# Self-attention values on 32x32 diagonal tiles with a row-sum column, in a one-layer perceiver kernel

## What is computed

```python
def _L0_attn_ref(x, ...):              # B = 128, L = 32, D = 256, H = 16 heads, HD = 16
    q = rms_norm(x, qn_scale) @ q_w.T + q_b
    k = rms_norm(x, kn_scale) @ k_w.T + k_b
    v = x @ v_w.T + v_b
    ...                                 # split in heads, rotary on q and k
    scores = jnp.einsum('bhqd,bhkd->bhqk', q, k) * scale
    weights = jax.nn.sigmoid(scores)
    weights = weights / (jnp.sum(weights, axis=-1, keepdims=True) + EPS_RENORM)
    attn = jnp.einsum('bhqk,bhkd->bhqd', weights, v)
    attn = attn.transpose(0, 2, 1, 3).reshape(B, L, D)
    return attn @ o_w.T + o_b
```

## Time and profile before

| | before |
|---|---|
| median of 3 runs | 1345.84 us (1345.80 to 1345.89) |
| the profiled execution | 1344.86 us |
| its span in the trace | 1343.0 us |
| one body in the steady part | 36.73 us |
| busy in the span: PE, DVE, ACT, POOL | 86%, 70%, 65%, 42% |

### The profile page before, as it was taken

One profiled execution on the slowest core, in us unless ns is written; L12 is line 12 of the kernel. 1 busy time (PEld: TensorE's weight loads), 2 busy tenths in 40 slices (PEclk: granted clock), 3 DMA queues, 4 the chain that ended last, 5 costly groups with the idle time before them and its releaser, 6 DMA issues.

```text
span 1343.0 us, 37302 instructions
## 1 busy us (share of the span) xinstructions
PE 1157.5 (86%) x14033; PEld 936.5 (70%) x14033; DVE 945.0 (70%) x2523; ACT 872.4 (65%) x2443; POOL 569.7 (42%) x1045
## 2 busy tenths in 40 slices
PE   6898889888888898889888888988898888864797
PEld 5676777767767777777767767767777677742697
DVE  3667777777777777777777777877777777763121
ACT  3676767777777667767777777667677777632131
POOL 1244454455444444444454444444444554431121
PEclk9899999999999999999999999999999999975899
DMA  6414211111211111111111111111111111000474
GB/s 148 126 47 144 84 57 43 51 54 51 52 40 45 49 52 47 50 47 39 46 48 50 49 30 50 49 49 46 50 40 39 48 48 45 14 9 13 115 225 153
DMA packets 71904, 81.93 MB, mean 61 GB/s; under 512 B 16987, under 2 KB 50732, under 8 KB 71728
## 3 DMA queue, kind: packets, MB, share of 16 engines
q1 hardware_dynamic: 65280, 75.19, 19.3%
q0 software_dynamic: 3200, 3.71, 0.8%
q10 hardware_dynamic: 3248, 0.66, 0.2%
HBM read 64.79 MB, written 16.56 MB: 61 GB/s over the span
## 4 chain that ended last, share of the span: by engine, by line
DVE 33%; PE 31%; ACT 20%; issue 9%; POOL 6%; SPq 0%; DVEq 0%; DMA 0%; ACTq 0%; POOLq 0%
ACT prob L739 8%; ACT wbd L799 4%; PE score L444 4%; PE vps L411 4%; PE kps L401 4%; DVE prob L974 4%; ACT qz L728 3%; DVE nmx L963 3%; PE shared L477 3%; PE shared L532 3%; PE shared L523 3%; PE score L670 3%; PE score L684 3%; DVE pr L1116 3%; POOL ctx_p L1273 2%
## 5 line engine op out<-in xcount | busy, mean ns | idle before, releaser
L739 ACT ACTIVATE prob<-score,nmx 128x257 f32<-128x257 f32 x512 | 236.2, 476 | 175.8 <-DVE nmx L963 175.0
L401 PE MATMUL kps<-ctx_p,wk_p 128*128 128x256 f32 x1536 | 213.6, 289 | 0.2 <-POOL ctx_p L1273 0.2
L411 PE MATMUL vps<-wv_p,ctx_p 128*128 128x256 f32 x1536 | 212.7, 288 | 0.0
L1273 POOL TENSOR_TENSOR ctx_p<-ctxT,ctx_p 128x512 fp32r<-128x512 f32 x128 | 152.1, 1188 | 119.8 <-ACT ctx_p L755 119.8
L411 PEld LDWEIGHTS vps<-wv_p,ctx_p 128*128 128x128 f32 x1536 | 192.6, 192 | 12.4 <-issue 12.4
L401 PEld LDWEIGHTS kps<-ctx_p,wk_p 128*128 128x128 f32 x1536 | 195.4, 192 | 5.4 <-issue 2.3
L963 DVE TENSOR_REDUCE nmx<-score 128x2 f32<-128x514 f32 x256 | 163.1, 679 | 15.7 <-PE score L428 15.7
L1291 POOL TENSOR_TENSOR plast<-const,prob 128x128 f32<-128x128 f32 x128 | 64.1, 501 | 257.7 <-DVE prob L974 257.7
L974 DVE TENSOR_SCALAR prob<-prob,rsum 128x257 f32<-128x257 f32 x512 | 158.3, 352 | 9.0
L444 PE MATMUL score<-const,prob 128*128 128x128 f32 x1024 | 145.7, 280 | 7.5 <-DVE prob L974 3.5
L444 PEld LDWEIGHTS score<-const,prob 128*128 128x128 f32 x1024 | 114.1, 142 | 44.4 <-DVE prob L974 28.6
(11 more groups left out here) (163 smaller groups left out, 2188.4 us busy)
## 6 DMA issues: line engine op xcount, KB each, us to landing
ctxT<-in_ctxT SPq DMA_DIRECT2D x128, 257.0 KB, 3.0
w<-in_w SPq DMA_DIRECT2D x16, 1024.0 KB, 9.7
xq<-in_x SPq DMA_DIRECT2D x32, 128.0 KB, 3.3
xr<-in_x SPq DMA_DIRECT2D x32, 128.0 KB, 2.5
qbd<-qkT SPq DMA_DIRECT2D x256, 16.0 KB, 1.8
out<-row SPq DMA_DIRECT2D x32, 128.0 KB, 1.9
slots<-row SPq DMA_DIRECT2D x10, 257.0 KB, 5.6
x_a<-slots SPq DMA_DIRECT2D x8, 129.0 KB, 2.1
```

Of the source, the lines that this page charges most:

```text
L401: last = mm(kps[:, c, :], wk_p[:, x, n, c * P:(c + 1) * P], ctx_p[:, g, y, n, :], start=(n, x) == (0, LO), stop=(n, y) == (C - 1, LO))
L411: last = mm(vps[:, c, :], ctx_p[:, g, x, n, c * P:(c + 1) * P], wv_p[:, y, n, :], start=(n, x) == (0, LO), stop=(n, y) == (C - 1, LO))
L739: last = af(prob[:, m, :], score[:, m, 0:S], ACT.Exp, bias=nmx[:, m:m + 1], scale=1.0, accum_out=esum[:, m:m + 1])
L1273: g.tensor_tensor(ctx_p[:, g_, LO, :, :], ctxT[:, r, :, g_, 0:SM], ctx_p[:, g_, HI, :, :].bitcast(F32), ALU.subtract).then_inc(s["ctx_part ...
```

## The change

The block-diagonal matrix `wbd`, the sums by ones and the selection of even and odd heads go. `v2` becomes `v2a`: for each head 16 values and a column of ones. PE multiplies, for each head and each sequence, the 32x32 block of `th` (the weights are loaded from it as it stands) with the 32x17 block of `v2a` on the diagonal tile (rows 32j, columns 32j of the array) and gets, with tokens on partitions, the 16 values and the sum of each head in 17 columns of `shared`. DVE adds the epsilon, inverts 128x16 sums and multiplies (`att2n`). PE transposes `att2n` into `spare`, and ACT copies it to `att2`, from where the projection goes on as before.

```diff
-            def weight_sums(t):
-                pe.wait_ge(s["sig_done"], TB * (t + 1))
...
-            def weighted_values2(t):
+            def self_values(t):
+                pe.wait_ge(s["sig_flat"], t + 1)
                 pe.wait_ge(s["v2_done"], t + 1)
...
+                for h in range(H):
+                    for j in range(TB):
+                        rows = slice(32 * j, 32 * j + 32)
+                        last = mm(shared[rows, h * (HD + 1):(h + 1) * (HD + 1)], th[rows, h * L:(h + 1) * L], v2a[rows, h, :],
                                   start=True, stop=True)
                 last.then_inc(s["pv2_ps"], 1)
...
-                    (1, 2): s2 and (lambda: (turn("sm_step", 2 * (t2 + 1)), weight_sums(t2))),
-                    (1, 3): s2 and (lambda: (turn("ext2_step", 2 * (t2 + 1)), weighted_values2(t2))),
+                    (1, 2): s2 and (lambda: (turn("att2n_done", t2 + 1), self_values(t2))),
                     (2, 0): s1 and (lambda: (turn("qk_done", t1 + 1), project_qk(t1))),
+                    (2, 1): s2 and (lambda: (spare_free(xa, i, 2), transpose_rows(att2n, "att2n_done", t2, "at2_ps", spare_c))),
...
             # ScalarE
-                    if j == 2 and s2:
-                        act.wait_ge(s["o2_ps"], t2)
-                        even_heads(att2, sh_pair[:, :, 0, :], "pv2_ps", t2 + 1, "ext2_step")
-                    if j == 1 and s2:
-                        sigmoid_blocks(t2, (2,))
+                    if j == 2 and s2:
+                        act.wait_ge(s["o2_ps"], t2)
+                        copy_rows(att2[:, :, :], spare_c, "at2_ps", t2, "att2_done")
-                    if j == 0 and s2:
-                        sigmoid_blocks(t2, (0, 1))
...
             # VectorE
-            def sigmoid_block(t, j):
-            def sums2(t):
-            def extract2(t):
...
+            def inverse2(t):
+                dve.wait_ge(s["pv2_ps"], t + 1)
+                v.tensor_scalar(ssum[:, :], sh_heads[:, :, HD], 2e-8, None, ALU.add).then_inc(s["ssum_step"], 1)
+                dve.wait_ge(s["ssum_step"], 2 * t + 1)
+                v.reciprocal(rsum2[:, :], ssum[:, :]).then_inc(s["ssum_step"], 1)
+            def weigh2(t):
+                dve.wait_ge(s["ssum_step"], 2 * t + 2)
+                dve.wait_ge(s["at2_ps"], t)
+                v.tensor_tensor(att2n[:, :].rearrange("p (h d) -> p h d", d=HD), sh_heads[:, :, 0:HD],
+                                rsum2[:, :].unsqueeze(2).to_broadcast([P, H, HD]), ALU.mult).then_inc(s["att2n_done"], 1)
```

More of the change, by code:

```diff
@@ L142, in build @@
         qbd2 = sb("qbd2", [P, C, HH, P])
-        v2 = sb("v2", [P, D])
+        v2a = sb("v2a", [P, H, HD + 1])
         th, tabs, sneg = (sb(n, [P, 2 * D]) for n in ("th", "tabs", "sneg"))
-        wbd = sb("wbd", [P, H, P])
-        ssum, att2 = sb("ssum", [P, C, P]), sb("att2", [P, C, P])
+        ssum, rsum2 = sb("ssum", [P, H]), sb("rsum2", [P, H])
+        att2n, att2 = sb("att2n", [P, D]), sb("att2", [P, C, P])
         row = sb("row", [P, ROW])
@@ L188, in build @@
         counts = gather[:, 0, 0, 0:E]
-        sh_pair = shared[:, :].rearrange("p (c g n) -> p c g n", c=C, g=2)
+        sh_heads = shared[:, 0:H * (HD + 1)].rearrange("p (h d) -> p h d", d=HD + 1)
         names = """const_in wq_in wkv_in weights_in bf_consts scaled zeroed klast_done vlast_done last_ps
@@ L517, in scores2 @@
                 last.then_inc(s["s2_ps"], 1)
-            def weight_sums(t):
-                pe.wait_ge(s["sig_done"], TB * (t + 1))
-                for c in range(C):
-                    for g in range(4):
-                        last = mm(shared[32 * g:32 * g + 32, c * D:(c + 1) * D], k["ones"][:, 0:32],
-                                  wbd[:, 8 * c + 2 * g:8 * c + 2 * g + 2, :].rearrange("p h n -> p (h n)"),
-                                  start=True, stop=True)
-                last.then_inc(s["sm_ps"], 1)
-            def weighted_values2(t):
-                pe.wait_ge(s["v2_done"], t + 1)
-                for c in range(C):
-                    for g in range(4):
-                        last = mm(shared[32 * g:32 * g + 32, c * D:(c + 1) * D], v2[:, c * P + 32 * g:c * P + 32 * g + 32],
-                                  wbd[:, 8 * c + 2 * g:8 * c + 2 * g + 2, :].rearrange("p h n -> p (h n)"),
+            def self_values(t):
+                pe.wait_ge(s["sig_flat"], t + 1)
+                pe.wait_ge(s["v2_done"], t + 1)
+                if once(t):
+                    pe.wait_ge(s["zeroed"], 2)
+                for h in range(H):
+                    for j in range(TB):
+                        rows = slice(32 * j, 32 * j + 32)
+                        last = mm(shared[rows, h * (HD + 1):(h + 1) * (HD + 1)], th[rows, h * L:(h + 1) * L], v2a[rows, h, :],
                                   start=True, stop=True)
@@ L790, in sigmoid_exp @@
                 af(sneg[:, :], sneg[:, :], ACT.Exp, scale=float(-SCALE)).then_inc(s["sneg_exp"], 1)
-            def sigmoid_blocks(t, batches):
-                if once(t):
-                    act.wait_ge(s["zeroed"], 2)
-                act.wait_ge(s["sig_flat"], t + 1)
-                for j in batches:
-                    b = slice(32 * j, 32 * j + 32)
-                    af(wbd[b, :, b], th[b, :].rearrange("p (h q) -> p h q", h=H), ACT.Copy).then_inc(s["sig_done"], 1)
             def gate_exp(t):
@@ L912, in setup @@
                     v.memset(qbd2[:], 0.0).then_inc(s["zeroed"], 1)
[L913 removed]
+                    v.memset(v2a[:, :, HD:HD + 1], 1.0).then_inc(s["zeroed"], 1)
                 if j == 1:
@@ L1162, in body @@
                         norm1(t1)
-                    if j == 2 and s2:
-                        weigh2(t2)
                     if j == 2 and s1:
@@ L1179, in body @@
                         residual1(t1)
-                    if j == 1 and s2:
-                        sigmoid_block(t2, 3)
-                        sums2(t2)
                     if j == 2 and s1:
@@ L1200, in body @@
                     if j == 1 and s2:
-                        inverse2(t2, 0)
-                        extract2(t2)
-                        inverse2(t2, 1)
+                        inverse2(t2)
+                        weigh2(t2)
                     if j == 2 and s2:
```

27 lines of the change are left out of this document (5 added, 22 removed).

## The result

The changed kernel takes 1335.20 us, the median of 5 runs (1330.20 to 1336.11), beside 1345.89 us of 5 runs of the kernel before (1345.80 to 1346.71). The ratio is 0.9907, with a 95% interval of 0.9884 to 0.9930: faster by 10.7 us, where the forecast was 1300, faster by 45.6. The sign holds, and the size does not.

What follows compares the result with a forecast made beforehand. A ring of waits, with no engine full, was taken to bound the kernel; 1.36 us in each of 30 bodies (40.8) plus the drain made 45.6 us, giving 1300 us. The range of 8 in 10 was 1278 to 1338.

Steps and rivals of the forecast that it cites:

- The ring of waits: Steady body of 36.74 us: no engine fills it (PE 32.80), so what counts is which engine is late at which step.
- the walk: From the new step to L1030 in a steady body: 1.36 us earlier, carried on by an untouched 7.06 us to L483.
- Its rule: Steady body: the gain is 3.41 us less the length of the new step, 1.36 us with a step of 2.05.
- the length of the step: PE, new step to L444: 128 matmuls at 14.8 ns plus 0.15 for the change of form, 2.05 us.
- DVE's additions: DVE before L492: addition, inversion (0.25) and product, some 0.95 us with gaps, ending at 693.5 before L492 at 694.01.
- the drain: Last two bodies, clock at half: gains of 1.4 us in the body before last and 3.4 in the last.
- the start: Work up to the first step of the loop: the forecast gave it no gain, and the removed memset no price.
- a floor from start to start: New step: about 25 ns per matmul, so 3.35 us; a body gains 0.06, about 1340 us; chance 0.12.
- Serial tiles: New step: diagonal tiles go one after the other, 5.0 us; a body loses 1.6, 1402 us; chance 0.08.
- Slow issue: New step: PE's instructions come too slowly for a burst of 256, costing 0.7 us a body; 1321 us; chance 0.12.
- The short step: New step: 17 columns make it 1.36 us or less; a body gains 2.05, 1278 us; chance 0.08.
- the cap of 2.05: Gain of a body in us with a step of 1.36 or less, where ACT sets L770 at 691.54.

Runs made afterwards that it cites:

- again: The changed kernel itself, not one instruction different, run once more on another chip: 1281.8 us, ratio 0.9526.
- the memset: The changed kernel with the removed zeroing of `wbd` (128x2048) put back on DVE in the first body, its tile unused: 1287.9 us.
- split: The changed kernel with its step in two halves, heads 8 to 15 moved behind the transposes of batch 1: 1275.4 us, ratio 0.9477.
- half_heads: The changed kernel with heads 8 to 15 left out of the new step, 64 matmuls instead of 128: 1263.9 us.
- Q: A chip with long gaps: the changed kernel took 1336.2 us there, and with its step in two halves 1301.8 (single runs).
- R: A chip with long gaps: the changed kernel took 1342.2 us there, and with its step in four pieces 1291.5 (single runs).

## Why the prediction was right and wrong

**What bounds the kernel: right.** The ring of waits was read rightly, and the walk through it holds. Its rule, that a body gains 3.41 us less the length of the step, gives 0.92 for the step of 2.49 and was measured at 36.73 - 35.75 = 0.98; for the 1.70 of again it gives 1.71, measured 36.73 - 34.93 = 1.80. The exponentials start 0.79 us after DVE's first maxima do (652.01), as foreseen 0.7, and the maxima of batch 2 wait for L428 and the evacuation of q and k for L492 (again, ACT and DVE):

```profile
652.80 0.48 ACT L734 ACTIVATE prob<-score,nmx 128x257 f32<-128x257 f32 x1 [1.20 <-DVE nmx L945]
...
659.17 0.17 DVE L1039 TENSOR_SCALAR ssum<-shared 128x16 f32<-128x16 f32 x1
659.37 0.25 DVE L1041 RECIPROCAL rsum<-ssum 128x16 f32<-128x16 f32 x1
659.66 0.42 DVE L1046 TENSOR_TENSOR att2n<-shared,rsum 128x256 f32<-128x256 f32 x1
660.80 1.29 DVE L945 TENSOR_REDUCE nmx<-score 128x2 f32<-128x514 f32 x2 [0.72 <-PE score L428]
662.36 0.75 DVE L1012 SCALAR_TENSOR_TENSOR qk<-shared,rrms,r_qk 128x512 f32<-128x512 f32 x1 [0.27 <-PE shared L492]
```

**DVE's additions: right.** 0.25 us was taken for the inversion of 128x16 and is what it takes; all three end at 660.08, 0.6 before L492. The transposes and the copy of `att2n` cost nothing beside a cross-attention, as said: PE waits for them 1.0 and 1.3 us in the whole span, in the drain.

**The length of the step: the term that was mis-sized.** It was taken as 2.05 us of steady matmuls. It is 8.5 ns for each matmul, near the lower end (14.8 ns of L459, halved for fewer columns), plus gaps: 1.70 us with the short ones and 2.49 with the long ones. The forecast's own band for the step, 1.5 to 2.6, held both. With 2.49 in the rule the sum is 30 x 0.92 + 4.8 = 32.4, a time of 1313, and 13 of the 35 us of the miss are explained.

**The term that wasn't there: the granted clock.** The prediction looked at the clock only in the drain and let the steady part run at the full level because it had done so before. On the chip of the result it fell behind the new step in 22 of 29 bodies, and some 29 us went there. This is the step that failed: a term of 29 us that the sum had at nothing. With the 13 above, less 5.7 and 0.8 that the start and the drain gave beyond the forecast, it makes the 35 us. That 1335.2 lies inside the range of 1278 to 1338 is luck, since the upper end of the range stood for a floor from start to start, which the rows refute. The rows of before could have raised the question, for PE is busy for 32.80 of the 36.74 us of a body, and a stretch at half speed lengthens it. They couldn't give the answer, since the same instructions keep the full clock on three of the six chips.

**The drain and the start.** The drain was put at 4.8 us and gives 5.6. The last body gains 5.4 (from L515 to L477 14.6 us before, 9.2 after) and not 3.4, in part since the step at half clock takes 2.9 us to the transposes and not 4.1; the last body with a cross-attention, with its gaps and its stretch at 1.2 GHz, loses 1.3. The start was given nothing and gives 5.7; the memset was worth 5.2 in its experiment. The terms together: forecast 40.8 + 4.8 = 45.6; measured on the chip of the result -1.5 + 5.6 + 5.7 = 9.7 of span; on the chip of again 50.5 + 6.8 + 6.4 = 63.7.

**The rivals.** (1) The floor near 25 ns is refuted: 8.5 ns from start to start. The Trainium skill's statement ("TensorE: Matmul & The Clock Gate", section "Wait — 56ns, not 53.3ns?") that there are never less than about 25 ns from one start to the next does not hold across the four diagonal tiles in this trace; on one tile the distance is 34 ns, which is above it. (2) Serial tiles are refuted by the same number, with four row groups in one PSUM bank on different partitions; the rule of the Trainium skill ("TensorEngine Tiling (Array Packing)", section "Restrictions and Gotchas"), that different row tiles can't access the same PSUM bank at the same time, did not bind here. (3) Slow issue was named, with 0.7 us in a body. Gaps put down to issue are real, and the step is about 0.8 us longer where they are long than where they are short. Its second effect, on the clock, was what nobody priced. (4) The short step came true for the matmuls and not for the step. In split and half_heads, where it is in force, a body gains 2.36 us instead of the cap of 2.05. The cap was counted from ACT's copies behind y1T; in split ACT's copy of the probabilities, L767, starts 2.18 us after the step does (654.82 to 657.00), not 2.44.

**What stays open.** What the two gaps are made of: the profile calls them issue, they come at a certain small matmul of the step, no instruction packet goes with them, and neither the length of the burst nor the waits put in behind it changed the first of them. Why three chips have them long and three short isn't shown either. And which of gap, small form and chip is needed for the fall of the clock can't be told apart fully: the long gaps and the falls always came on the same chips, all runs that changed the form alone fell on a chip where the clock doesn't fall anyway, and no gap was made by hand on such a chip. What is shown is that on a chip with long gaps the fall depends on how the step is cut: 22 stretches whole, 7 in halves (Q), and 24 whole, 2 in quarters (R).

## What to carry to other kernels

Cut a burst of small tiled matmuls in pieces and put full-size work between them: in two pieces it saved 6.5 to 34 us on the three chips where it was run. When a change replaces a few large matmuls by many small ones in a kernel where PE is nearly full, price three things: the matmuls, gaps between them, and half a clock for PE's work behind them. Run such a change on several chips before it is judged; one chip would have said 0.8% here and another 4.8%.

## What the runs showed of the hardware

- Chips differ in the gaps that PE has in a burst of small matmuls: the same kernel took 1281.8 to 1283.6 us on three chips (gaps of 0.14 and 0.27 us from start to start) and 1336.2 to 1342.2 on three others (0.54 and 0.66 to 0.69), while the kernel before took 1345 to 1346 on all of them.
- PE's instructions come in blocks: with 256 small matmuls and their weight loads in a row, PE stood still for 0.6 to 2.7 us in 29 of 30 steps, at a place that moves as a block of 256 instructions does, and went on 1.2 to 1.6 us after an instruction packet of 16384 bytes had ended.
- 32x32 tiles on the diagonal run side by side at 8.5 ns from start to start at 2.4 GHz, in one PSUM bank. 32 columns instead of 17 made no difference that can be seen (a step of about 1.7 us both times).
- Behind the step with its two long gaps (0.38 and 0.50 us idle in the row) TensorE's clock fell to 1.2 GHz 22 to 24 times in 29 bodies. With one gap of 0.43 us and larger work between the pieces it fell twice, once of them behind the step, and with the stop of 1.28 us between large matmuls 8 times.
- An operation of 1.76 us on DVE in the start put the first step of the loop off by 5.2 us, at a mean clock of 0.93 instead of 0.98 up to there.
